# Gate and up by Strassen's seven products on halves of 1024 tokens, down added up in SBUF, weight-block sums on GpSimd

## The reference

```python
x = x + einsum('bct,bcd->bdt', x, w0[idx_a]) + bias[idx_a][:, :, None]        # layer 0
lin = lambda v, W, A, B: v @ W + (v @ A[idx_a]) @ B[idx_a]
x = x + lin(silu(lin(x, Wg, Ag, Bg)) * lin(x, Wu, Au, Bu), Wd, Ad, Bd)        # layer 1: 512 -> 2048 -> 512
x = x + x @ W2.T + ((x @ A2[idx_b].T) @ B2[idx_b].T) * s[idx_b]               # layer 2
x = x + einsum('bct,bcd->bdt', x, w3[idx_c])                                  # layer 3
```

## Time and profile before

| | |
|---|---|
| span of the profiled execution | 798.9 us |
| runs | 799.77, 802.61, 803.45 us |
| TensorE (PE) busy | 762.9 us, 95% |
| TensorE weight load (PEld) busy | 643.5 us |
| VectorE (DVE) busy | 388.7 us, 49% |
| ScalarE (ACT) busy | 292.8 us, 37% |
| GpSimd (POOL) busy | 228.1 us, 29% |
| mean granted TensorE clock | 0.991 |
| DMA | 90.65 MB, mean 113 GB/s |

### The profile page before, as it was taken

How to read it: one execution, slowest core, us unless ns; L and a number is a source line. 1 busy time by engine, 2 the same in 40 slices (tenths; PEclk the granted TensorE clock), 3 DMA queues, 4 the chain that set the end, 5 groups by cost and what they waited for, 6 DMA issues and landing times. The chain is left out here.

```text
span 798.9 us, 12005 instructions
## 1 busy us (share of the span) xinstructions
PE 762.9 (95%) x3820; PEld 643.5 (81%) x3820; DVE 388.7 (49%) x669; ACT 292.8 (37%) x552; POOL 228.1 (29%) x465
## 2 busy tenths in 40 slices
PE   3799969999899999999999999999999999999997
PEld 2688868888788888888888888888888878878885
DVE  6565424333565444444565444445444344346665
ACT  3444223333434343333344433343334343323332
POOL 5356652343312433433232433222233000000000
PEclk9899989999999999999999999999999999999999
DMA  7944433346324433433333343442343432212212
GB/s 167 202 143 135 147 93 106 107 133 212 91 72 133 121 107 107 134 107 107 111 110 120 103 129 115 134 158 66 105 132 106 103 82 79 92 54 80 106 53 79
DMA packets 123856, 90.65 MB, mean 113 GB/s; under 512 B 37168, under 2 KB 102704, under 8 KB 123824
## 3 DMA queue, kind: packets, MB, share of 16 engines
q1 hardware_dynamic: 109984, 68.75, 28.6%
q0 software_dynamic: 7808, 19.93, 8.8%
q10 hardware_dynamic: 6032, 1.58, 0.9%
HBM read 77.65 MB, written 4.19 MB: 102 GB/s over the span
## 5 line engine op out<-in xcount | busy, mean ns | idle before, releaser
L974 PE MATMUL bank<-XT,gu 128*128 128x512 f32 (+1 forms) x1536 | 377.7, 395 | 9.4 <-DVE gu L149 4.1
L974 PEld LDWEIGHTS bank<-XT,gu 128*128 128x128 f32 x1536 | 283.3, 189 | 67.0 <-issue 9.5
L1017 PE MATMUL bank<-wds,hs 128*128 128x512 f32 x768 | 187.3, 392 | 0.0
L149 DVE TENSOR_TENSOR gu<-stage,gu 128x1024 fp32r<-128x1024 f32 x64 | 78.5, 1227 | 188.2 <-ACT gu L145 187.8
L1017 PEld LDWEIGHTS bank<-wds,hs 128*128 128x128 f32 x768 | 139.8, 188 | 27.7
L138 ACT ACTIVATE gu<-stage 128x1024 fp32r<-128x1024 f32 x64 | 67.8, 1059 | 161.2 <-DMA stage<-in_L_cond_Wd_dram 157.7
L388 POOL DMA_INDIRECT braw<-in_L_cond_Bg_dram,boffs x64 | 70.9, 1107 | 172.9 <-DVE gu L149 150.9
L543 ACT ACTIVATE hs<-hid 128x512 fp32r<-128x512 f32 x64 | 40.5, 632 | 153.7 <-DVE hid L797 143.2
L404 POOL COPY adsel<-ad_raw 128x32 f32 x256 | 42.5, 213 | 178.5 <-DVE wds L791 165.3
L979 PEld LDWEIGHTS bank<-UT,gu 128*128 128x128 f32 x512 | 78.1, 189 | 9.9
L979 PE MATMUL bank<-UT,gu 128*128 128x256 f32 (+1 forms) x512 | 81.0, 281 | 0.0
(11 more groups left out here) (109 smaller groups left out, 543.3 us busy)
## 6 DMA issues: line engine op xcount, KB each, us to landing
stage<-in_L_cond_Wg_dram SPq DMA_DIRECT2D x64, 256.0 KB
stage<-in_L_cond_Wu_dram SPq DMA_DIRECT2D x64, 256.0 KB
stage<-in_L_cond_Wd_dram SPq DMA_DIRECT2D x64, 256.0 KB
xh<-X SPq DMA_DIRECT2D x8, 512.0 KB, 3.7
out_dram<-y SPq DMA_DIRECT2D x16, 256.0 KB, 2.0
X<-x1s SPq DMA_DIRECT2D x14, 256.0 KB
X<-in_x_dram SPq DMA_DIRECT2D x3, 1024.0 KB
X<-in_x_dram SPq DMA_DIRECT2D x4, 256.0 KB
```

The lines of the kernel that those rows point to most:

```text
L149: return nc.vector.tensor_tensor(gu[s][:, 1, at, :], src, gu[s][:, 0, at, :].bitcast(f32), ALU.subtract)
L974: nc.tensor.matmul(psum[:, :], gu[s][:, a, KT * j + k, :], XT[:, b, k, ds(c, TOK)], start=(k == 0 and n == 0), stop=False)
L1017: last = nc.tensor.matmul(psD[j][:, :], hs[s][:, a, j * P:(j + 1) * P], wds[s][:, b, :], start=(first and n == 0), stop=False)
```

## The change

Tokens are now worked in two halves of 1024 (HALVES, 8 pairs each), hidden features in eight tiles of 256 (UNITS). A unit is one tile of 256 for one half; there are 16 units. Input features, hidden features and tokens of a unit are each cut in two, and the 2x2 block product of gate (and of up) is made by the Strassen-Winograd form: seven block products in place of eight. Each block product (`product`) is 2 x 3 matmuls of 512 columns. It needs sums of weight blocks S1 to S4 and of token blocks T1 to T4, and sums of the products.

- GpSimd makes S1 to S4 for every weight tile (`combine`: four TENSOR_TENSOR of 128x256 float32 each), into SC, one buffer for gate and up. Its loop over units is `p_combine(u)`, `gather_b(2u+2)`, `g_combine(u+1)`, `select_ad(u)`, `gather_b(2u+3)`. `gather_b` now fills one buffer BR, without a ring, and waits until both pieces of the last one were split (`s_bl`).
- VectorE makes T1 to T4 once for each half (`xc_rest`), and the sums of products for each gate and up: `sum_u2`, `sum_u3`, `sum_half22`, `sum_c22`, `sum_c21`, `sum_c12`, each 128x512. ScalarE copies the first product out of PSUM (`p1_copy`).
- `down` of a unit is eight groups of six matmuls, in two PSUM banks in turn, and each is added into X1 at once (`evict`, one VectorE operation of 128x512 for each pair of tokens and unit).
- A unit has a gate window and an up window. In each, TensorE runs the first three products, `c11_product`, two downs of the unit before with one `ranks`, `c21_product`, two more downs and one `ranks`, and `c12_product`.
- Layer 0 and the transposes of the first half come before the main loop, those of the second half inside unit 0. X1 of the second half is parked in DRAM. Layers 2 and 3 no longer form a block of their own; `lora_down` now runs beside them, through one PSUM bank psE.
- The weights are read twice in all.

```diff
+                def gather_b(b):
+                    unit, rows = b // 2, (bg_rows, bu_rows)[b % 2]
+                    if b:
+                        pool.wait_ge(s_bl, 2 * b)
...
+                    for q in range(HQ):
...
+                        nc.gpsimd.indirect_dma_start(
+                            BR[:, q, :], None, rows,
+                            bass.IndirectOffsetOnAxis(boffs[:, at:at + 1].bitcast(u32), 0),
+                            element_offset=i * QT).then_inc(s_br[q // 2], 16)
+                def combine(t, w, ready, last):
+                    pool.wait_ge(ready[0], ready[1])
+                    if last[1]:
+                        pool.wait_ge(s_wl[last[0]], last[1])
...
+                    nc.gpsimd.tensor_tensor(s1, a21, a22, ALU.add).then_inc(s_comb[t], 1)
+                    nc.gpsimd.tensor_tensor(s3, a11, a21, ALU.subtract)
+                    pool.wait_ge(s_comb[t], 3 * w + 1)
+                    nc.gpsimd.tensor_tensor(s2, s1, a11, ALU.subtract).then_inc(s_comb[t], 1)
+                    pool.wait_ge(s_comb[t], 3 * w + 2)
+                    nc.gpsimd.tensor_tensor(s4, a12, s2, ALU.subtract).then_inc(s_comb[t], 1)
...
+                for h in range(HALVES):
+                    cols = adapters(h)
+                    for i in range(UNITS):
+                        unit = UNITS * h + i
+                        p_combine(h, i)
+                        if unit + 1 < ALL:
+                            gather_b(2 * unit + 2)
+                            g_combine(unit + 1)
+                        if h + 1 < HALVES and i + 1 == UNITS:
+                            a_combine(h + 1)
+                        select_ad(unit, cols)
+                        if unit + 1 < ALL:
+                            gather_b(2 * unit + 3)
...
+                def w_high(t, w, n_before, ready):
...
+                    nc.scalar.activation(WC[:, t, A11:A12 + 1, 0, :, :],
+                                         raw[:, :, 0:P].rearrange("p (s k) f -> p s k f", s=2), ACT.Copy)
+                    nc.scalar.activation(WC[:, t, A22, 0, :, :], raw[:, 2:4, P:QT], ACT.Copy).then_inc(s_wh[t], 1)
+                    act.wait_ge(s_comb[t], 3 * w + 3)
+                    nc.scalar.activation(WC[:, t, S1:S4 + 1, 0, :, :],
+                                         SC[:, :, :].rearrange("p s (k f) -> p s k f", k=2), ACT.Copy).then_inc(s_wh[t], 1)
...
+                def gate_window(h, i):
+                    n, unit = nG(h, i), UNITS * h + i
+                    if i:
+                        sum_c12(n - 1, tmp[:, 1, :])
+                        gated(unit - 1, n - 1, 1, 4, 4)
...
+                    sum_u2(n)
+                    if i:
+                        wd_low(unit - 1)
+                        hs_low(unit - 1, 0, 1, 4)
+                    b_low(2 * unit, 1)
+                    w_low(U, wP(h, i))
+                    if i:
+                        ad_low(unit - 1)
...
+                    sum_u3(n)
+                    sum_half22(n, tmp[:, 3, :], 1)
+                    if i:
+                        evict(unit - 1, 0)
+                        evict(unit - 1, 1)
...
+                    sum_c22(n, hid[:, 3, :])
+                    sum_c21(n, hid[:, 2, :])
+                    if i:
+                        evict(unit - 1, 2)
...
+                    b_low(2 * unit + 1, 0)
+                    if i:
+                        evict(unit - 1, 3)
+                def up_window(h, i):
+                    n, unit = nP(h, i), UNITS * h + i
+                    sum_c12(n - 1, hid[:, 1, :])
+                    b_low(2 * unit + 1, 1)
...
+                    sum_u2(n)
+                    if unit + 1 < ALL:
+                        w_low(G, unit + 1)
...
+                    gated(unit, n, 0, 1, 0)
+                    sum_u3(n)
+                    sum_half22(n, tmp[:, 3, :], 1)
+                    hs_low(unit, 0, 0, 1)
+                    if i:
+                        evict(unit - 1, 4)
+                        evict(unit - 1, 5)
...
...
+                def product(psum, t, left, right, first):
+                    for k in range(2):
+                        for n, (a, b) in enumerate(THREE):
+                            last = nc.tensor.matmul(psum[:, :], WC[:, t, left, a, k, :], XC[:, right, b, k, :],
+                                                    start=(first and k == 0 and n == 0), stop=(k == 1 and n == 2),
+                                                    skip_group_check=not first)
+                def first_products(n, t):
...
+                    product(psA, t, A11, B11, True).then_inc(s_prod, 1)
+                    product(psB, t, S2, T2, True).then_inc(s_prod, 1)
+                    product(psC, t, S1, T1, True).then_inc(s_prod, 1)
+                def c11_product(n, t, b):
+                    pe.wait_ge(s_p1, n + 1)
+                    product(psA, t, A12, B21, False)
+                    pe.wait_ge(s_bl, 2 * b + 1)
+                    lora(psA, 0, t, 0, False).then_inc(s_prod, 1)
+                    pe.wait_ge(s_add, 6 * n + 1)
+                    product(psB, t, S3, T3, False).then_inc(s_prod, 1)
+                def c21_product(n, t, b, order):
+                    pe.wait_ge(s_bl, 2 * b + 2)
+                    if t == G:
+                        pe.wait_ge(s_silu, order)
+                    else:
+                        pe.wait_ge(s_hid, order)
+                    lora(psA, 1, t, 1, True).then_inc(s_prod, 1)
+                    pe.wait_ge(s_add, 6 * n + 2)
+                    product(psB, t, A22, T4, False)
+                    lora(psB, 1, t, 0, False).then_inc(s_prod, 1)
+                def c12_product(n, t):
+                    pe.wait_ge(s_add, 6 * n + 3)
+                    product(psC, t, S4, B22, False)
+                    lora(psC, 0, t, 1, False).then_inc(s_prod, 1)
+                def down(unit, j):
+                    g = HP * unit + j
...
+                    if g >= 2:
+                        pe.wait_ge(s_evict, g - 1)
...
+                def ranks(unit, q):
+                    if q == 0:
+                        pe.wait_ge(s_adl, unit + 1)
...
+                def downs(unit, at):
...
+                    down(unit, 2 * at)
+                    down(unit, 2 * at + 1)
+                    ranks(unit, at)
```

More of the change, by code:

```diff
@@ L142, in b_high @@
[L142 to L155, removed]
@@ L880, in _, with tail @@
+                def tail(h):
+                    n, unit = nP(h, UNITS - 1), UNITS * h + UNITS - 1
+                    sum_c12(n, tmp[:, 1, :])
+                    gated(unit, n, 1, 4, 4)
+                    wd_low(unit)
+                    hs_low(unit, 0, 1, 4)
+                    ad_low(unit)
+                    for j in range(HP):
+                        evict(unit, j)
+                    ud_mask(h)
                 rows_of_ranks()
@@ new lines, in _ @@
+                n, unit = LASTP, ALL - 1
+                sum_c12(n, tmp[:, 1, :])
+                gated(unit, n, 1, 4, 4)
+                wd_low(unit)
+                hs_low(unit, 0, 1, 4)
+                ad_low(unit)
+                ud_low(0)
+                bd_low(0)
+                bd_low(1)
+                for j in range(HP):
+                    evict(unit, j)
+                    if j >= 2:
+                        table_low(j - 2)
+                ud_mask(1)
+                ud_low(1)
@@ L958, in select @@
-                def select(g, j, bank):
-                    pe.wait_ge(s_ul, g + 1)
-                    if later(g, 1) and j == 1:
-                        pe.wait_ge(s_um, 2 * g + 1)
-                    for a in range(2):
-                        at = 2 * j + 1 - a
-                        last = nc.tensor.matmul(bank[:, :], moves[:, at:at + 2, :].rearrange("p a m -> p (a m)"),
-                                                us[:, a, :], start=(a == 0), stop=(a == 1))
-                    last.then_inc(s_sel, 1)
@@ new lines, in lora @@
+                def lora(psum, f, j, tok, first):
+                    for q in range(2):
+                        for a in range(2):
+                            last = nc.tensor.matmul(psum[:, q * QT:(q + 1) * QT], BL[:, a, 2 * tok + q, f * P:(f + 1) * P],
+                                                    UT[:, j, (2 * tok + q) * QT:(2 * tok + q + 1) * QT],
+                                                    start=(first and q == 0 and a == 0), stop=(q == 1 and a == 1),
+                                                    skip_group_check=True)
+                    return last
```

2040 lines of the change are left out of this document (1083 added, 957 removed).

## The result

The changed kernel takes 1121.89 us (median of four runs, 1120.43 to 1122.56); the kernel before took 803.03 beside it. The ratio is 1.3998, 95% interval 1.3954 to 1.4042: 40% slower. The span of the profiled execution is 1118.6 us.

The account below looks back on a forecast made before the run. The prediction took TensorE's gapless matmuls to bound the kernel before. Start 60, unit 0 56, 14 units of 51.9 (727), turn 44, unit 8 44 and end 134 gave a 1065 us span; with 3.7 added, 1068, range 955 to 1150.

Parts of the forecast that it names:

- What bounds it before, and what can be saved: Main loop before: gapless TensorE matmuls; a unit's own matmuls take 35.9 us against 38.6, net 36 us less at most.
- The new wait: Each window: gathers and GpSimd sums stand between b_low and w_low, 10.4 us; TensorE idles 7.3 (gate), 4.2 (up).
- GpSimd's sum: One 128x256 two-input sum on GpSimd: 0.6 us taken, bounds 0.38 and 0.78; four take 2.6 us with waits.
- The rival of contention: VectorE's two-input operations hold up GpSimd's sums, 1.2 us each in 31 windows: 1142 us in all, chance 0.13.
- The clock: TensorE's clock falls after idleness: 2.7 us lost per gate window, half, 1.4, per up window; granted clock 0.85 to 0.9.
- Unit 8: First unit of the second half, without downs: 41 + 2.7, taken as 44 us.
- Units 0 and 1: First two units: unit 0 at 56 us, without downs but with layer 0 work on VectorE; unit 1 at 52.
- The end: From the last unit to the finish, with downs, tables, six lora_down rounds and the later layers: 134 us.
- Start and turn: Time before unit 0, 60 us, and between the halves, 44 us; hand schedules, a tenth each way allowed.
- the steady units: Main-loop units outside the start and turn: 51.9 us each with the clock's loss, 14 of them making 727 us.

Follow-up runs that it names:

- e1: Changed kernel with only GpSimd's queue reordered, each window's weight sums issued before the adapter gathers: 905.0 us.
- e6: Changed kernel with all sums ahead of gathers, layer 3's gathers spread two a unit, last token copy and second lora_down moved: 848.7 us, 1.059 times the kernel before.
- e5: Changed kernel with only the sums of up's weights ahead of their window's gathers, gate's sums left behind theirs: 990.7 us.
- e7: Changed kernel with no sums on GpSimd; VectorE makes them at the head of w_low, gathers as they were: 882.2 us.
- e2: Changed kernel with matmuls that compute nothing put where TensorE waits in gate and up windows: 1093.9 us.
- e4: Changed kernel with layer 3's 16 weight gathers issued two a unit in the second half, behind select_ad: 1104.8 us.

## Why the prediction was right, point by point

The forecast was 1068 us in 955 to 1150; 1121.9 was measured, 54 above.

- **What bounds it before, and what can be saved.** Right. In e1 and e6 a unit takes 35.9 us, the predicted count, where four steps take 38.6.
- **The new wait.** Right, and nearly to the number: gathers 5.1 forecast, 4.95 measured (412.13 to 417.08); from b_low's end to w_low's end 10.4 forecast, 10.5 and 10.3 measured. TensorE idle 7.3 and 4.2 forecast, 7.0 and 3.8 measured. Gate window 28.0 with the clock, 27.5 measured; up 23.9 and 23.6. e1 and e5 show that the order in the queue is the cause.
- **GpSimd's sum.** 0.6 us taken, 0.74 to 0.76 measured as means by line, near the upper bound of 0.78; four take 2.9 us in place of 2.6. A shorter stretch of gathers and shorter handoffs made up for most of it. By the Trainium skill's figure (GPSIMD Engine Reference, "Performance versus the Vector engine") the estimate was 0.55 us and some dispatch; the trace has 0.75, and the measurement decides.
- **The rival of contention.** It didn't come true, for the reason given against it: in the changed kernel VectorE mostly waits while GpSimd sums. What it fears does exist. In e1 the two meet: of 136 sums, 115 last 0.71 to 0.76 us and 14 last 1.07, and each that lasts over 1 us stands beside a VectorE operation with both inputs in SBUF. The larger price is VectorE's: its product L928 takes 2.46 us in place of 0.69. In e7, with no sums on GpSimd, the same product takes 0.70 in the mean. The Trainium skill (GPSIMD Engine Reference, "Specifications") lists GpSimd's SBUF interfaces as shared with VectorE, with contention where VectorE has two SBUF inputs; the trace of e1 agrees, with the 2.46 us above.
- **The clock.** Right in the mean: 0.865, forecast 0.85 to 0.9. Its two parts were not. 3.8 us of idleness was taken as a fall in half of the cases, but all 14 up windows that waited show it (six matmuls as one block in 2.54 to 2.85 us, 1.55 at full clock). And such a fall costs less than 2.7. Beyond the 17.9 us of a window and its wait, an up window takes 1.8 us more and a gate window 2.6. The trace shows where the difference lies: behind the wait the up window's first four matmuls still go at nearly full speed (0.71 us below, 1.22 at 422.99). So the 1.4 taken for an up window came near 1.8 by luck. e2 puts what a full clock gives back at 3.7 us a unit, where 4.1 were forecast.

```profile
396.70 0.71 PE L1259 MATMUL bank<-UT,BL 128*128 128x256 f32 x4 [3.80 <-DVE hid L922]
397.25 2.74 PE L1251 MATMUL bank<-XC,WC 128*128 128x512 f32 x6
```

- **Unit 8, 24 us too short: the step that was mis-sized.** The forecast counted for it only the missing downs. It left out GpSimd's queue between the halves: 16 gathers of layer 3's weights, 20.0 us from 564.75 to 584.76, ahead of `p_combine(1, 0)`. e4 shows 17 of the 24.
- **Units 0 and 1, 15 and 11 us too short.** Left out in unit 0: 16 index values that GpSimd reads into registers ahead of up's first sums. These reads (L392) stand 0.55 us apart, from 77.5 to 86.8, partly beside the gathers; what is left of them behind the last gather are the 5.9 us before the first sum (below). Where the rest of the 15 us goes stays open. In unit 1 the first ranks waited 18.0 us for `xr_copy` of the last pair, which stands behind ScalarE's wait for the sums. Most of that is the sums' chain again: with GpSimd's order alone changed (e1) the wait is 8.9, and with the copy moved ahead too (e6) 6.0.

```profile
80.15 0.95 POOL L361 DMA_INDIRECT BR<-in_L_cond_Bu_dram,boffs  x1 [0.30 <-issue]
87.04 0.72 POOL L374 TENSOR_TENSOR SC<-RW 128x256 f32<-128x256 f32 x1 [5.94 <-issue]
```

- **The end, 15 us too short.** `lora_down` of a duo goes through one bank psE, and the second one waits 2.0 us for VectorE to empty it, in four duos. With the second behind the rank input (e6) it waits 0.6, and the end takes 137 us, not 149.
- **Start and turn.** 66.5 and 42.4 for 60 and 44: the turn within the tenth given, the start just over it, and its cause stays open. Start, turn and end together are 257.5 for 238.

Two errors of opposite sign make the 54 us. Outside the steady units the forecast was 70 us too short, and the steady units were 16 too long: 10 from 0.8 us a unit, and 6 because unit 15's up window, which takes 17.9 us without a wait, was counted as a full one. That the total came within 54 us is in part luck. Of the 70 us the runs show the greater part to be instructions in an in-order queue ahead of something that TensorE needed: layer 3's gathers, the sums ahead of `xr_copy`, the index reads, the second `lora_down`. The prediction had followed this rule for the steady unit and had not read the same queues at the edges of the loops.

## What to carry to other kernels

Before giving an engine new work on the way to TensorE, write down what stands ahead of it in that engine's queue and what that waits for: here a gather that waited for the same window put 5 us in front of 3 us of sums, and one reorder was worth 217 us of 1122. A saving of TensorE work (7% of a unit) has to pay for its stages at the edges: even in e6 the start, unit 0, the turn and the end hold 82 us of idle time, where the whole kernel before had 36, and the matmuls saved are worth 36. When TensorE waits for several us at a time, count the slow matmuls behind each wait as well, here 3.7 us in a unit of 51.

## What the runs showed of the hardware that was not expected

A GpSimd TENSOR_TENSOR of 128x256 float32 takes 0.74 to 0.76 us in the mean against VectorE's 0.43 for the same tile. When it runs beside VectorE operations with both inputs in SBUF, those pay more than GpSimd does: 0.69 us becomes 2.46, and the last sum goes from 0.74 to 1.07 (e1).

The length of one idle time doesn't settle whether the clock falls. It fell behind each wait of 3.8 us or more in the up windows, it fell behind 3.12 us and not behind 3.17 in the kernel before, and in e2 matmuls were slow behind one wait of 1.75 us and not behind another of 1.74.

Reading 16 values into GpSimd's registers takes some 8 to 9 us of its queue, 0.55 us each, but it can run beside indirect gathers. Ahead of unit 0 5.9 us of it stood behind the last gather. Ahead of unit 8 all of it ran beside layer 3's gathers: the first sum starts 0.03 us after the last of them.
